# Fused two-layer block on one core: another order of the items between the blocks in the second shared-key attention stage

## The reference

```
qp = layernorm(x) @ Wq.T
idx = argmax(qp @ ctx.T, axis=-1)        # the nearest context row of each row
mem = ctx[idx]                           # gathered rows
mk, mv = split(mem @ Wkv.T)              # one key and value head, 16 wide
attn = softmax(heads(qp) @ mk.T / 4)     # 16 query heads on that one key head
x = x + tanh(g) * ((attn @ mv) @ Wc.T)
```

## Time and profile before

| what | value |
|---|---|
| median of 3 runs | 4641.18 us (4638.0 to 4642.87) |
| the profiled execution | 4657.65 us |
| its span, first to last instruction | 4655.8 us |
| busy time of TensorE, matmuls | 4037.3 us (87%) |
| busy time of VectorE | 2849.2 us (61%) |
| busy time of ScalarE | 2016.2 us (43%) |
| busy time of GpSimd | 1003.0 us (22%) |
| mean granted clock of TensorE | 0.922 of 2.4 GHz |
| first and last copy of the keys in stage C (L518) | 1494.8 and 2346.9 us |

### The profile page before, as it was taken

How to read it: one execution, slowest core, us unless ns; L and a number is a source line. 1 busy time by engine, 2 the same in 40 slices (tenths; PEclk the granted TensorE clock), 3 DMA queues, 4 the chain that set the end, 5 groups by cost and what they waited for, 6 DMA issues and landing times. The chain is left out here.

```text
span 4655.8 us, 87718 instructions
## 1 busy us (share of the span) xinstructions
PE 4037.3 (87%) x29034; PEld 2742.1 (59%) x29034; DVE 2849.2 (61%) x6892; ACT 2016.2 (43%) x3617; POOL 1003.0 (22%) x1850
## 2 busy tenths in 40 slices
PE   4999999555555899999978999999979999999999
PEld 2555555233333555555545555555568888888888
DVE  5666666599996777777745666666653333333333
ACT  2555555355553455555544445544422222222222
POOL 2433443000000333233314343433420000000000
PEclk8999999766666899999988999999989999999999
DMA  2000000000000000000000000000020000000000
GB/s 91 12 11 9 11 11 7 24 0 0 0 0 13 10 12 9 9 9 9 9 9 6 19 18 18 18 18 18 20 83 28 14 27 14 27 14 27 14 27 14
DMA packets 79349, 80.26 MB, mean 17 GB/s; under 512 B 4880, under 2 KB 76560, under 8 KB 79248
## 3 DMA queue, kind: packets, MB, share of 16 engines
q1 hardware_dynamic: 79248, 78.91, 5.3%
HBM read 53.73 MB, written 25.17 MB: 17 GB/s over the span
## 5 line engine op out<-in xcount | busy, mean ns | idle before, releaser
L632 DVE TENSOR_REDUCE a_neg_max<-psum 128x2 f32<-128x512 f32 x512 | 329.2, 685 | 207.0 <-PE psum L802 205.7
L1301 DVE TENSOR_REDUCE d_neg_max<-psum 128x2 f32<-128x256 f32 (+1 forms) x512 | 261.4, 553 | 285.9 <-PE psum L1464 284.0
L632 DVE TENSOR_REDUCE c_neg_max<-psum 128x2 f32<-128x512 f32 x512 | 329.0, 685 | 133.6 <-PE psum L802 132.6
L533 ACT ACTIVATE c_exps<-psum 128x512 f32<-128x512 f32 x512 | 277.9, 595 | 247.1 <-PE psum L824 247.0
L533 ACT ACTIVATE a_exps<-psum 128x512 f32<-128x512 f32 x512 | 278.0, 594 | 210.9 <-PE psum L824 210.5
L1205 ACT ACTIVATE d_exps<-psum 128x512 f32<-128x512 f32 (+1 forms) x512 | 223.3, 488 | 289.4 <-PE psum L1491 289.3
L2306 PE MATMUL psum<-e_hidden_l,e_e_l_high 128*128 128x512 f32 x1024 | 321.0, 395 | 2.8 <-POOL e_e_l_low L2079 2.8
L821 PE MATMUL psum<-a_q_by_parity,a_k_stationary 32*128 32x512 f32 x1536 | 274.8, 437 | 23.2 <-ACT a_exps L533 22.4
L802 PE MATMUL psum<-c_k_by_parity,c_q_high_low 32*128 32x512 f32 x1536 | 289.9, 443 | 5.4 <-DVE c_neg_max L632 5.4
L802 PE MATMUL psum<-a_k_by_parity,a_q_high_low 32*128 32x512 f32 x1536 | 271.5, 443 | 10.2 <-DVE a_neg_max L632 10.0
L821 PE MATMUL psum<-c_q_by_parity,c_k_stationary 32*128 32x512 f32 x1536 | 266.1, 439 | 3.6 <-ACT c_exps L533 2.8
(11 more groups left out here) (437 smaller groups left out, 10393.1 us busy)
## 6 DMA issues: line engine op xcount, KB each, us to landing
x_all<-in_x_dram SPq DMA_DIRECT2D x4, 2048.0 KB, 15.9
a_ctx<-in_ctx_t_dram SPq DMA_DIRECT2D x32, 256.0 KB, 2.7
c_ctx<-in_ctx_t_dram SPq DMA_DIRECT2D x32, 256.0 KB, 2.6
x_rows<-d_x SPq DMA_DIRECT2D x32, 256.0 KB, 2.2
out_dram<-d_y SPq DMA_DIRECT2D x32, 256.0 KB, 2.3
e_x<-x_rows SPq DMA_DIRECT2D x16, 512.0 KB, 4.3
e_y<-out_dram SPq DMA_DIRECT2D x16, 512.0 KB, 3.7
out_dram<-e_y SPq DMA_DIRECT2D x16, 512.0 KB, 3.2
```

What stands on the lines that cost most here:

```text
L533: s_.activation(EX[:, t], st_bank[t % 3], ACT.Exp).then_inc(exp_done, 1)
L632: v.tensor_reduce(NM[:, :, t, r, m], sc_bank[u % 3].rearrange("p (e k) -> p e k", e=2), AX.X, ALU.max, negate=True).then_inc(sc_used, 1)
L1301: v.tensor_reduce(NM[:, :, t, r, m], sc_bank[u % 3][:, 0:512 if t else 256].rearrange("p (e k) -> p e k", e=2), AX.X, ALU.max, negate=True ...
```

## The change

Three strings, the orders of stage C on TensorE, ScalarE and VectorE, are written anew. In TensorE's order v1- and NM1- come one block after another behind x0 and x1; p0 stands behind NM1-; p1 to p4 come one to two blocks later than before; NM0 and OT- follow x5; p3 and PR- follow v0 behind x6; and p5 stands behind x7, just ahead of T0, where it was behind x5. VectorE takes p2 behind s9 (it was behind s5) and p5 behind s15. Items, their contents and GpSimd's and SyncE's programs stay as they are; since the two banks are given out in TensorE's order, some items change their bank.

Besides, six waits on freed() in TensorE's program become evicted(), which leaves the wait out where the named item had the same bank as the new one; use() waits for that bank anyway. This holds for stage A too, whose strings stay.

```
--- before.py
+++ after.py
@@ -34,15 +34,15 @@
 PARTS = ((0, 0), (0, 1), (1, 0))
 PAIR_PE = {
     "A": "x0 NM1- v1- x1 p0 T1- x2 p1 x3 OT- x4 p2 x5 NM0 v0 x6 PR- x7 T0",
-    "C": "x0 p0 NM1- x1 p1 x2 p2 x3 v1- x4 p4 T1- p3 x5 p5 OT- x6 v0 NM0 x7 PR- T0",
+    "C": "x0 v1- x1 NM1- p0 x2 p1 T1- x3 p2 x4 p4 x5 NM0 OT- x6 v0 p3 PR- x7 p5 T0",
 }
 PAIR_ACT = {
     "A": "t0 t1 NM1- v1- t2 t3 p0 t4 t5 p1 t6 t7 OT- t8 t9 p2 t10 t11 NM0 v0 t12 t13 t14 t15",
-    "C": "t0 t1 p0 NM1- t2 t3 p1 t4 t5 t6 t7 v1- t8 t9 p4 p3 t10 t11 p5 OT- t12 t13 v0 NM0 t14 t15",
+    "C": "t0 t1 v1- t2 t3 NM1- p0 t4 t5 p1 t6 t7 t8 t9 p4 t10 t11 NM0 OT- t12 t13 v0 p3 t14 t15 p5",
 }
 PAIR_DVE = {
     "A": "s0 s1 s2 s3 s4 s5 T1- s6 s7 NM0 s8 s9 N p2 s10 s11 s12 s13 PR- s14 s15 NM1 T0",
-    "C": "s0 s1 s2 s3 s4 s5 p2 s6 s7 NM0 s8 s9 T1- s10 s11 p5 N s12 s13 s14 s15 NM1 PR- T0",
+    "C": "s0 s1 s2 s3 s4 s5 T1- s6 s7 NM0 s8 s9 p2 s10 s11 N s12 s13 PR- s14 s15 p5 NM1 T0",
 }
 
 
@@ -732,6 +732,10 @@
                         pe.wait_ge(free[k], w)
                     return k
 
+                def evicted(source, s, x):
+                    if place(*source)[0] != place(s, x)[0]:
+                        freed(pe, *source)
+
                 def transpose_rows(w, src):
                     for cc in range(DC):
                         for t in range(2):
@@ -744,16 +748,16 @@
                     if k == 0:
                         pe.wait_ge(xn_ready, b + 1)
                     elif k == 1:
-                        freed(pe, s, "p0")
+                        evicted((s, "p0"), s, x)
                     elif k == 2:
                         pe.wait_ge(ctx_in[n], 16 * (j + 1))
                         if gathered:
-                            freed(pe, s, "p1")
+                            evicted((s, "p1"), s, x)
                     elif k == 3:
                         pe.wait_ge(prep_step, 3 * b + 3)
                     elif k == 5:
-                        freed(pe, s, "p3")
-                        freed(pe, s, "p4")
+                        evicted((s, "p3"), s, x)
+                        evicted((s, "p4"), s, x)
                     f = use(s, x)
                     w = w_bank[f]
                     if k == 0:
@@ -858,18 +862,18 @@
                         prep(int(x[1]), s)
                     elif x in ("T0", "T1-"):
                         k = int(x[1])
-                        freed(pe, s, "v0" if x == "T0" else "v1-")
+                        evicted((s, "v0" if x == "T0" else "v1-"), s, x)
                         f = use(s, x)
                         for u in range(4):
                             t_ = tr(w_bank[f][:, u * P:(u + 1) * P], OV[:, k, u * P:(u + 1) * P], self.IDF[:])
                         t_.then_inc(full[f], 1)
                     elif x == "OT-":
-                        freed(pe, at(s, -1), "T0")
-                        freed(pe, s, "T1-")
+                        evicted((at(s, -1), "T0"), s, x)
+                        evicted((s, "T1-"), s, x)
                         f = use(s, x)
                         transpose_rows(w_bank[f], O).then_inc(full[f], 1)
                     elif x == "PR-":
-                        freed(pe, s, "OT-")
+                        evicted((s, "OT-"), s, x)
                         f = use(s, x)
                         for t in range(2):
                             for cc in range(DC):
```

## The result

The changed kernel takes 4777.68 us (median of 4 runs, 4761.71 to 4792.75) against 4642.02 us before (4 runs, 4638.0 to 4643.16): a ratio of 1.029, 95% interval 1.0262 to 1.0317, so 136 us slower. The forecast was 4765 us, range 4700 to 4805. The profiled execution took 4792.75 us, the slowest of the four; 4657.65 us was that of before.

What follows compares the result with a forecast made beforehand. TensorE was taken to bound stage C. Its step grows from 27.48 to 30.2 us, +82 us over thirty steps, plus 42 us for clock drops: +124 us on the median 4641.18 gives 4765 us, range 4700 to 4805.

Steps and rivals of the forecast that it cites:

- Redundant waits: Dropped waits in stages A and C: hidden by running matmuls, gain taken as 0, at most 46 us.
- The three old waits: TensorE's stage C waits at NM1-, PR- and p5: all 3.0 us a step go, down to 24.5.
- The keys' chain: From p5 through ScalarE and GpSimd's key copies to the next x0: TensorE waits 3.7 us a step.
- The search's bank ahead of NM0: TensorE's NM0 waits until VectorE's p2 search frees its bank: 0.85 us a step.
- x6's wait for s10: TensorE's x6 block waits for VectorE's s10, delayed by the p2 search: 0.5 us a step.
- PR-, 0.45: PR- shares a bank with v0, only p3 between, and waits for ScalarE's copy: 0.45 us a step.
- p1, 0.2: p1, one block behind p0, waits while ScalarE does two exps, NM1- and p0: estimated 0.2 us a step.
- The new step without the clock: Stage C step of 24.5 us work plus the new waits: 30.2 us, against 27.48 before.
- The clock: TensorE's new stop in stage C drops its granted clock nearly every step: 1.4 us each, 42 us in all.
- Rival 2: VectorE's NM1 operations slow GpSimd's keys, so the wait grows by 0.8 us a step: 4789 us, chance 0.08.
- Rival 3: VectorE's new waits, 0.85 and 0.5 us a step in stage C, don't show: 4725 us, chance 0.05.
- Rivals 1 and 4: 1: waits without a clock drop, 4723 us, chance 0.17; 4: keys one batch ahead, unchanged (0.04) or 4611 us (0.06).

Runs made afterwards that it cites:

- third order: Changed kernel's three stage C orders rewritten again, p5 behind x6, six us ahead of the next x0: 4597.66 us, ratio 0.9917 to the kernel before.
- slower keys: Kernel before with two extra GpSimd additions at the head of keys() in stage C: 4651.75 us; the same in the changed kernel: 4837.14 us.
- the filled kernel: Changed kernel with 12 extra matmuls ahead of x0's first in stage C, run while TensorE waits for the keys: 4714.25 us.

## Why the prediction was right, by its own steps

- *Redundant waits, taken as 0.* Not contradicted: the old orders with the dropped waits leave 0.3% open, and only a part of C's dropped waits is in that run.
- *The three old waits go.* Right; none of them is in the profile after.
- *The keys' chain, 3.7 us a step.* Right to 0.1: chain of 5.9 us, x0 on at 6.0 after p5, due at 2.3. The profile prints 3.17 since the first matmul of t0 runs for 0.49 of the time. Lengthening the chain lengthened the step by 2.0 us in the changed kernel and by 0.3 in the one before, shifting p5 forward removed the loss, and p5 late alone brought 99 of 136 us.
- *The search's bank ahead of NM0, 0.85.* 0.58 measured. *x6's wait for s10, 0.5:* the block took from 2060.93 to 2062.51, 1.58 instead of 1.13, so 0.45. *PR-, 0.45:* 10.7 / 25 = 0.43. *p1, 0.2:* 6.2 / 25 = 0.25.
- *The new step without the clock:* 30.2 forecast, 30.0 measured with the wait filled. The text on the change counts p4 among the items that come later; it kept its place behind x4, and the prediction reckoned with that.
- *The clock, 1.4 us a step, 42 us.* The term that was mis-sized: 2.1 us a step, 63 us, by filling the wait. I had one drop's price (1.6) from stage D and took some off, because part of it would fall on the stop. But a drop in stage C holds the lower clock for longer: 0.06 x 2 x 30.1 = 3.6 us in the step of D, 4.5 us on average here. And little of it falls on the stop: the clock was still 1.00 up to 2040.60, 0.8 us before x0 went on. For each us at 1.2 GHz the two cost about the same, 1.6 / 3.6 = 0.44 and 2.15 / 4.5 = 0.48. The term was inside the ends of 0 and 3.2 that were kept for the range.
- *Rival 2, keys held up by VectorE.* Not seen: casts and copies take 0.40 and 0.94 as before. It is VectorE that gets slower beside them: in the changed kernel's NM1 its last two small operations (L651, L653) took 0.45 and 0.44 us, in the NM0 of the third order at 2026.83, with GpSimd idle, 0.20 and 0.23. That GpSimd can be the slower one too shows only in small sizes and with the old orders: 510 ns against 481 for L424, and with slower keys 456 against 394 for the cast. *Rival 3* had half a point: NM0's wait was smaller by a third. *Rivals 1 and 4* fell with the granted clock of 0.93 and the wait for L430.

The sum is then 74 us of waits and some 63 of clock, 137, for 136 measured. That it closes is no proof of its own, since the 63 is the filled kernel against the changed one and the filled kernel is 72 above before; what is independent are the 74 us from the steps of the trace. And the forecast of 124 came as near as it did partly because its errors offset each other: the waits were 8 us too large, the clock 21 too small.

## What to carry to other kernels

In a pipeline that is ordered by hand, write down for each item the time from its start to the last effect that somebody waits for, through all engines, also those whose order isn't edited; here GpSimd's 3.4 us behind p5 decided, and GpSimd has no string. Here TensorE's new stop of 3.7 us cost 2.1 us more than its length, so such a stop must be worth more than the short ones that it replaces; harmless matmuls in it gave these 2.1 us back, but not the wait, and the filled kernel was still 72 us slower than the one before. And the order is worth searching by slack, the time between an item's last effect and its first use: the same work ran in 4598, 4642 and 4778 us.

## What was not expected of the hardware

Twelve added matmuls a step, 2.99 us of work each time, made the changed kernel 63 us faster, more than the 42 expected. And the runs of an unchanged kernel differ by up to 0.8%, going with the granted clock of the execution: 17 runs of the kernel before ranged from 4621.58 us (mean clock 0.932) to 4660.05 us (0.922), so differences of some 0.2% between kernels need many runs here.
